# First phase in a new order: the next item's transpositions between the output products, spread and attention products between the value products

## The reference, cut to what matters

```python
q = split_heads(x @ Wq.T); k = split_heads(x @ Wk.T); v = split_heads(x @ Wv.T)   # x: layernormed
q = jax.nn.elu(q) + 1.0
k = jax.nn.elu(k) + 1.0
kv_state = jnp.einsum('bhnd,bhne->bhde', k, v)
k_state = k.sum(axis=2)
attn_out = jnp.einsum('bhnd,bhde->bhne', q, kv_state)
denom = jnp.maximum(jnp.einsum('bhnd,bhd->bhn', q, k_state), 1e-06)[..., None]
attn_out = (attn_out / denom).transpose(0, 2, 1, 3).reshape(b, s, d)
xp = jnp.pad(x, ((0, 0), (1, 1), (0, 0)))
local = xp[:, :-2, :] * conv_w[:, 0] + xp[:, 1:-1, :] * conv_w[:, 1] + xp[:, 2:, :] * conv_w[:, 2] + conv_b
return (attn_out + local) @ Wp.T + bp
```

## Time and profile before

| | us |
|---|---|
| median of three runs | 3675.85 |
| lowest and highest of them | 3665.65, 3680.14 |
| profiled execution | 3669.31 |
| its span | 3667.6 |
| of it TensorE busy | 3419.1 (93%) |
| VectorE busy | 2083.7 (57%) |
| ScalarE busy | 1344.5 (37%) |
| GpSimd busy | 815.0 (22%) |

### The profile page before, as it was taken

How to read it: one execution, slowest core, us unless ns; L and a number is a source line. 1 busy time by engine, 2 the same in 40 slices (tenths; PEclk the granted TensorE clock), 3 DMA queues, 4 the chain that set the end, 5 groups by cost and what they waited for, 6 DMA issues and landing times. The chain is left out here.

```text
span 3667.6 us, 42899 instructions
## 1 busy us (share of the span) xinstructions
PE 3419.1 (93%) x16304; PEld 2809.7 (77%) x16304; DVE 2083.7 (57%) x3935; ACT 1344.5 (37%) x2271; POOL 815.0 (22%) x740
## 2 busy tenths in 40 slices
PE   7999999999849999999999996899999999999798
PEld 6778787878638778877787775788888888888676
DVE  5565656565458888888888885322222223221676
ACT  4444444344235554555555543221111111211232
POOL 2223222232223332333333331000000000000244
PEclk9999999999879999999999998899999999999899
DMA  2010111011031111211121102100000000000343
GB/s 95 35 69 35 69 35 69 35 69 47 35 112 65 52 47 47 82 60 47 47 82 59 47 24 93 45 23 12 12 23 12 13 23 12 23 1 1 118 150 126
DMA packets 102348, 188.37 MB, mean 51 GB/s; under 512 B 6912, under 2 KB 13056, under 8 KB 102144
## 3 DMA queue, kind: packets, MB, share of 16 engines
q1 hardware_dynamic: 99840, 184.58, 14.5%
q10 hardware_dynamic: 2304, 1.05, 0.1%
HBM read 135.28 MB, written 50.33 MB: 51 GB/s over the span
## 5 line engine op out<-in xcount | busy, mean ns | idle before, releaser
L1536 ACT ACTIVATE c_gate<-c_g,c_bias 128x512 f32<-128x512 f32 x192 | 132.4, 689 | 803.1 <-PE c_g L102 803.1
L1555 DVE TENSOR_TENSOR c_gate<-c_gate 128x512 f32<-128x512 f32 x64 | 44.3, 692 | 599.7 <-ACT c_gate L1536 599.7
L1096 DVE TENSOR_TENSOR b_p_lo<-b_p_f,b_p_hi 128x512 fp32r<-128x512 f32 x256 | 255.5, 999 | 55.4 <-ACT b_p_hi L963 52.3
L955 ACT ACTIVATE b_p_f<-b_r,b_p_bias,b_p_scale 128x512 f32<-128x512 f32 x256 | 199.2, 778 | 216.3 <-PE b_r L102 212.6
L256 POOL TENSOR_TENSOR c_ln_sc<-c_ln_ve,minus_half 128x4 f32<-128x4 f32 x16 | 16.1, 1007 | 979.2 <-DVE c_ln_ve L249 979.2
L909 POOL TENSOR_TENSOR b_psum<-b_psum,b_p_f 128x512 f32<-128x512 f32 x128 | 171.2, 1338 | 126.4 <-ACT b_p_f L955 125.1
L1071 DVE CUSTOM_DVE_ANT_0 b_unused<-b_r,b_mask_row 128x512 bf16<-128x512 f32 x256 | 170.3, 683 | 1.2 <-issue 0.6
L963 ACT ACTIVATE b_p_hi<-b_p_f 128x512 fp32r<-128x512 f32 x256 | 161.5, 631 | 18.8 <-ACT b_p_f L955 1.1
L909 POOL TENSOR_TENSOR b_psum<-b_p_f 128x512 f32<-128x512 f32 x64 | 87.5, 1366 | 345.6 <-ACT b_p_f L955 192.5
L915 POOL TENSOR_TENSOR b_q_lo<-b_rope,b_q_hi 128x512 fp32r<-128x512 f32 x64 | 91.3, 1426 | 262.9 <-ACT b_q_hi L973 262.9
L419 POOL TENSOR_TENSOR a_res<-a_res,a_bp 128x512 f32<-128x512 f32 x64 | 81.8, 1308 | 299.9 <-DMA a_res<-in_x 299.9
(11 more groups left out here) (317 smaller groups left out, 10591.6 us busy)
## 6 DMA issues: line engine op xcount, KB each, us to landing
a_x<-in_x SPq DMA_DIRECT2D x16, 1024.0 KB, 8.0
a_res<-in_x SPq DMA_DIRECT2D x16, 1024.0 KB, 5.4
x<-a_res SPq DMA_DIRECT2D x16, 1024.0 KB, 4.3
b_mem<-in_ctx SPq DMA_DIRECT2D x16, 1024.0 KB, 7.8
b_x<-x SPq DMA_DIRECT2D x16, 1024.0 KB, 5.5
b_res<-x SPq DMA_DIRECT2D x16, 1024.0 KB, 5.5
x<-b_res SPq DMA_DIRECT2D x16, 1024.0 KB, 4.3
c_x<-x SPq DMA_DIRECT2D x16, 1024.0 KB, 5.6
```

The source lines that it names most:

```text
L955: act.activation(p_f[:, i, :], bank_of("st", j)[:, :], ACT.Exp, bias=p_bias[:, i:i + 1], scale=p_scale[:, i:i + 1]).then_inc(p_exp.sem, p_ ...
L1096: dve.tensor_tensor(p.low[:, i, :], p_f[:, i, :], p[:, i, :].high_f32(), ALU.subtract).then_inc(p_lo.sem, p_lo.unit)
L1536: act.activation(gate[:, j % 2, i, :], gating.banks[(3 * j + i) % 6][:, :], ACT.Tanh if g == "c" else ACT.Sigmoid, bias=bias[:, i, j:j + 1 ...
```

## The change

The change is a new order on all engines in the first phase; what is computed and the number of instructions of each kind stay.

- TensorE: the transpositions of the next item leave the head of the step. Two of them stand ahead of the first output block, two ahead of the third. They get a ring of their own with two banks (`turning`, names `a_t`), and the ring `second` has three banks instead of four. The first item's transpositions stand ahead of the pipeline. Spread and attention products of chunk c stand ahead of value block c.
- ScalarE: the copies of value blocks (`values`) stand between the spread copies and the high parts of z. High part and middle tap of the next item's chunk 0 stand ahead of the kv high part, those of chunks 1 to 3 behind it.
- VectorE: maximum and reciprocal follow each other directly; low parts and outer taps of the next item stand between the kv low part and the residual additions.
- SyncE: the load of the next x comes first in a step, the load of the residual second.

The core of the diff; helpers that only moved are left out:

```diff
+            turning = Ring(self.banks(ctx, "a_t", 2), [(tap2, c) for c in range(C)], B)
-            second = Ring(self.banks(ctx, "a_r", 4),
-                          [(tap2, c) for c in range(C)] + [e for c in range(C) for e in ((spread_sb, c, 1), (att_sb, c, 1))]
+            second = Ring(self.banks(ctx, "a_r", 3),
+                          [e for c in range(C) for e in ((spread_sb, c, 1), (att_sb, c, 1))]
                           + [(x1_sb, t, 1) for t in range(T)], B)
-            SPREAD, OUT = C, 3 * C
+            SPREAD, OUT = 0, 2 * C
...
                 def step(new, old):
+                    if following(new, B):
+                        load(sp, new.b + 1)
                     if old:
                         if old.b >= 1:
                             sp.wait_ge(stored.sem, stored.upto(old.b - 1))
                         sp.dma_start(res[:, :, :], self.token_rows(io["x"], old.b)).then_inc(res_in.sem, res_in.unit)
-                    if following(new, B):
-                        load(sp, new.b + 1)
...
-                    if old:
-                        for c in range(C):
+                    for c in range(C):
+                        if old:
                             spread_copy(c)
                             if c >= 1:
                                 z_high(c - 1)
+                        if new:
+                            values(c)
+                    if old:
                         z_high(C - 1)
...
+                    if following(new, B):
+                        tokens_high(new.b + 1, 0)
+                        middle_tap(new.b + 1, 0)
...
+                    if after:
+                        tokens_low(after, 1)
+                    if old:
+                        residual(old.b, 0)
+                    if after:
+                        outer_taps(after, 0)
+                        outer_taps(after, 1)
+                    if old:
+                        residual(old.b, 1)
+                    if after:
+                        tokens_low(after, 2)
+                        tokens_low(after, 3)
+                        outer_taps(after, 2)
...
-                    if old:
-                        for t in range(T):
+                    for t in range(T):
+                        if following(new, B) and t % 2 == 0:
+                            turn_x(new.b + 1, t)
+                            turn_x(new.b + 1, t + 1)
+                        if old:
                             if freed := second.freed(s, OUT + t):
                                 pe.wait_ge(*freed)
                             bank = second.bank(OUT + t)
...
+                def turn_x(b, c):
+                    if c == 0:
+                        pe.wait_ge(N.normed.sem, N.normed.upto(b))
+                    if freed := turning.freed(b, c):
+                        pe.wait_ge(*freed)
+                    self.turn(pe, turning.bank(c), x, c).then_inc(xT_ps.sem, xT_ps.unit)
+                for c in range(C):
+                    turn_x(0, c)
                 pipeline(B, step)
```

More of the change, by code:

```diff
@@ L461, in spread_copy, with values @@
                             act.wait_ge(z_lo.sem, z_lo.upto(old.b if c >= 2 else old.b - 1, c - 2 if c >= 2 else C + c - 2))
-                        act.activation(att[c % 2][:, :], second.banks[(SPREAD + 2 * c) % 4][:, :], ACT.Copy).then_inc(spread_sb.sem, spread_sb.unit)
+                        act.activation(att[c % 2][:, :], second.bank(SPREAD + 2 * c)[:, :], ACT.Copy).then_inc(spread_sb.sem, spread_sb.unit)
+                    def values(t):
+                        act.wait_ge(v_ps.sem, v_ps.upto(new.b, t))
+                        if t == 0:
+                            if new.b >= 1:
+                                act.wait_ge(kv_ps.sem, kv_ps.upto(new.b - 1))
+                        act.activation(v1[:, t, :, 0:P],
+                                               first.banks[(V + t) % 3][:, :].rearrange("p (c e) -> p c e", c=C), ACT.Copy).then_inc(v_sb.sem, v_sb.unit)
                     def z_high(c):
@@ L514, in step, with tokens_high, middle_tap @@
                                                 kv_f, ACT.Copy).then_inc(kv_hi.sem, kv_hi.unit)
+                    if following(new, B):
+                        for c in range(1, C):
+                            tokens_high(new.b + 1, c)
+                            middle_tap(new.b + 1, c)
+                def tokens_high(b, c):
+                    act.wait_ge(xT_ps.sem, xT_ps.upto(b, c))
+                    if c == 0 and b >= 1:
+                        act.wait_ge(kq_ps.sem, kq_ps.upto(b - 1))
+                    act.activation(xT.high[:, c, :], turning.bank(c)[:, :], ACT.Copy).then_inc(xT_hi.sem, xT_hi.unit)
+                def middle_tap(b, c):
+                    act.activation(local[b % 2][:, c, :], turning.bank(c)[:, :], ACT.Identity,
+                                   bias=conv_b[:, c:c + 1], scale=conv_w[:, c, 1:2]).then_inc(tap1.sem, tap1.unit)
+                for c in range(C):
+                    tokens_high(0, c)
+                    middle_tap(0, c)
                 pipeline(B, step)
@@ L560, in step @@
                     if new:
-                        taps(1)
+                        elu_back(0)
                         elu_back(1)
@@ L596, in step @@
                                                              bank[:, i, P:P + 1], None, ALU.mult).then_inc(kv_part.sem, kv_part.unit)
+                    after = new.b + 1 if following(new, B) else None
+                    if after:
+                        tokens_low(after, 0)
+                    if new:
                         dve.wait_ge(kv_hi.sem, kv_hi.upto(new.b))
@@ L600, in step @@
                         dve.tensor_tensor(both(kv[new.par].low), kv_f, both(kv[new.par].high).bitcast(F32), ALU.subtract).then_inc(kv_lo.sem, kv_lo.unit)
+                    if after:
+                        tokens_low(after, 1)
                     if old:
-                        for t in range(T):
-                            dve.wait_ge(res_bp.sem, res_bp.upto(old.b, t))
-                            dve.wait_ge(out_ps.sem, out_ps.upto(old.b, t))
-                            dve.tensor_tensor(res[:, t, :], second.banks[(OUT + t) % 4][:, :], res[:, t, :], ALU.add).then_inc(x1_sb.sem, x1_sb.unit)
+                        residual(old.b, 0)
@@ L606, in _, with residual @@
+                def residual(b, t):
+                    dve.wait_ge(res_bp.sem, res_bp.upto(b, t))
+                    dve.wait_ge(out_ps.sem, out_ps.upto(b, t))
+                    dve.tensor_tensor(res[:, t, :], second.bank(OUT + t)[:, :], res[:, t, :], ALU.add).then_inc(x1_sb.sem, x1_sb.unit)
+                for c in range(C):
+                    tokens_low(0, c)
+                    outer_taps(0, c)
                 pipeline(B, step)
@@ L613, in step @@
                     s = new.b if new else old.b + 1
-                    if new:
-                        for c in range(C):
-                            if freed := second.freed(s, c):
-                                pe.wait_ge(*freed)
-                            bank = second.bank(c)
-                            if c == 0:
-                                pe.wait_ge(N.normed.sem, N.normed.upto(new.b))
-                            self.turn(pe, bank, x, c).then_inc(xT_ps.sem, xT_ps.unit)
                     if old:
```

68 lines of the change are left out of this document (27 added, 41 removed).

## The result

| | before | after |
|---|---|---|
| median, us | 3674.97 (four runs, 3665.65 to 3680.14) | 3709.18 (four runs, 3707.69 to 3709.27) |
| profiled execution, us | 3669.31 | 3709.27 |

The changed kernel takes 1.0091 of the time before, 95% interval 1.0074 to 1.0109: slower by 0.9%, as forecast (3708). The interval holds no 1, so the sign is clear of the noise.

The account below looks back on a forecast made before the run. TensorE was taken to set the pace, losing 4.03 us of each 59.67 us pass. 3669.3 + 1.0 + 12.7 - 0.7 + 22.4 = 3704.7, stated as a median of 3708 us; range 3692 to 3720, 8 in 10 3672 to 3732.

Parts of the forecast that it names:

- start and second pass: First transpositions have only two banks, so two tap pairs (2.9 us) precede the fourth chunk; with the second pass, +1.0 us.
- last pass and drain: The last pass, which holds only the old item, was to stay as before: 0.
- What the change removes: Stops between key and value products, at the spread and attention products, go: up to 4.03 us a pass given back.
- Wait (a): Late value copies, z splits and normalisation delay the first query block; the fourth waits 0.7 us for its PSUM bank.
- Wait (b), (c): Late query chain starts kv masks 3.4 us behind key-value products; third and fourth transpositions await taps' banks, 4.2 us lost.
- The clock: TensorE runs about 8 products at 1.2 GHz behind the new stop: 1.6 us a pass, 22.4 us in all.
- The store and the loads: SyncE's later residual load delays GpSimd's bias additions, but value products cover that: costed at 0, 14 us if uncovered.
- Rival 1: The clock holds through the stop, all else as forecast: 3686 us, no change; chance 0.20.
- Rival 2: VectorE's chain to the taps is shorter: 3655 us, or 3614 if taps are wholly in time; chance 0.14.
- Rival 3: The clock falls deeply at each stop, 2.9 us a pass: 3726 us with the median's offset; chance 0.13.
- rival 4: The spread stretch still stops for its 2.8 us a pass: 3747 us; chance 0.04.

Follow-up runs that it names:

- interleaving alone: Kernel before with only spread and attention products ahead of each value block and ScalarE's value copies among them; 3633.19 us, ratio 0.9889 to before.
- statistics early: Changed kernel with the next item's normalisation statistics ahead of the last low part of z on VectorE; 3657.38 us, ratio 0.9956 to before.
- Later turns: Changed kernel with chunk 2's transpositions ahead of the fourth output block, chunk 3's behind it, VectorE's low part 3 behind residual 2; 3640.31 us, ratio 0.9907 to before.
- Taps before the residual: Changed kernel with residual addition 0 behind the first two pairs of taps on VectorE; 3690.64 us, ratio 1.0034 to before.
- the old order: Changed kernel with SyncE's loads in their old order, residual first, then next x; 3711.26 us, ratio 1.0100 to before.
- another start: Changed kernel with two fills of unused tiles on VectorE ahead of the first phase's very last residual addition; median 3706.66 us, ratio 1.0077 to before.
- both repairs: Changed kernel with the edits of Later turns and statistics early together; 3618.28 us, ratio 0.9837 to before.

## Why the prediction was right, point by point

The ledger of the two profiled executions, whose spans lie 39.9 us apart, against the forecast's 35.4:

| part | forecast | measured |
|---|---|---|
| start and second pass | +1.0 | +3.7 |
| the 14 passes, clock included | +34.4 | +29.0 |
| last pass and drain | 0 | -1.4 |
| rest | 0 | +8.6 |

- **What the change removes** held. No spread or attention product waits in any of the 14 passes, and the two waits of the earlier trace rows are gone. The interleaving alone brings 2.3 us of the 4.03 a pass; 1.06 us (9.3 + 5.6 in 14 passes) stays idle in its passes, for the reciprocal's low part, which was waited for before, and for the fourth query block, which is new.
- **Wait (a)**, forecast 0.7: the query products take 11.60 to 11.64 us instead of 10.88, 13 times. It comes with the interleaving alone (5.6 us, 13 times), and statistics early removes it, so its cause is shown: value copy, z high, z low, normalisation, first query block.
- **Wait (b), (c)**: masks 3.4 us behind the key-value products, measured 3.26; stop 4.2, measured 570.06 - 564.9 - 0.83 = 4.33. It is made up otherwise than forecast: 2.95 us up to the third transposition, and from there 2.21 us to the first product, 0.83 of it work at the full clock, where the forecast had a second wait of 1.0. The transpositions run slow, so that only 0.34 us of that wait is left between them. Later turns removes this stop alone, statistics early shortens it: the mechanism is shown from both ends.
- **The clock** is the term that was mis-sized in the passes. I took 1.6 us for 8 slow products behind each stop. Where eight are slow, that is the price (statistics early: passes of 60.1 us with eight against 58.5 without), but it is not paid at each stop. In ten passes only two or three are slow (570.06 to 571.06), and the second half of the outputs takes 6.25 us instead of 5.61; the last four have 10, 7, 5 and 12 slow ones. The mean is 0.97 us, so this term was 8.8 us too large over 14 passes. Taps before the residual shows that the size could not have been read from the length of the stop alone.
- **Start and second pass**, forecast +1.0. The stops ahead of the first key products (3.28 and 0.92 us) were foreseen, but the first key product starts 4.0 us later (34.61 against 30.59), where I had 2.9. I had not foreseen that nine products behind them would be slow (34.61 to 38.17): the key products of the first item take 12.99 us instead of 12.34. The second pass's denominator starts 1.2 us later than these two explain, where I had 0.9. And this pass has wait (a) already, 0.7 us, which I counted from the third pass on. Together the error is 2.7 us.
- **The store and the loads**, forecast 0: the old order gives the same pass, 61.73.
- **What the sum left untouched** was not untouched: the rest took 8.6 us more. I had costed it at nothing since no instruction of it changes. The counts of slow products show the clock in the second phase as its cause: 130 against 67, with nearly equal waits. The new order does not force them, since three kernels that keep it in the main (statistics early, another start, taps before the residual) took 2625.7, 2618.1 and 2622.2 us. Nor are they plain noise: the unedited kernels repeated their 2634.2 and 2625.9. Yet one kernel may vary as well, as the two groups of times of another start suggest. What picks one course or the other is not settled.

So 3708 against 3709.18 is closer than the sum deserves. The direction follows from the mechanism that the runs show; the closeness is luck. The clock in the passes was too dear by 8.8 us and the last pass by 1.4; stops 2.1, start 2.7 and rest 8.6 were too cheap, and 1.3 us lie in stages that this ledger does not separate. A slip of the sum is in it too: 60.55 - 59.67 = 0.88, times 14 is 12.3 us, not 12.7.

Rival 1 fell: the clock did drop at every stop, if less. (With a shorter stop, in statistics early, it held in ten passes of 14.) Rival 2 fell as well; every link of the chain came within 0.25 us. But its second number, 3614 for a change whose taps are in time, is what both repairs together give (3618.28). Rival 3 fell with the 0.97 us, and rival 4 with the spread stretch.

## What to carry to other kernels

When work is moved between engines' orders, take each wait that the new place needs and follow it through the queue of the engine that must answer it, with all that stands ahead there: here the gain on TensorE was sure, and two banks that VectorE freed late cost 4.3 us a pass, and the clock behind them 1.0, and ate it. A ring made shorter is gated by its last reader's place in line; where a moved consumer must wait, moving it one or two blocks further (later turns, 69 us less) or filling the answering engine's idle time (statistics early, 52 less) can be worth more than the change itself. Of these 52 us, 8.6 came from phases that the edit does not touch, so a whole time alone would have misled. And a change of several parts is to be taken apart: half of this one was worth -1.1%.

## What the runs showed of the hardware that was not expected

- **A stop and the clock behind it can trade.** With the stop 0.6 us shorter (first wait 2.11 us instead of 2.70), the slow products went from 56 to 71 in 14 passes and most passes stayed at 61.4 us. The Trainium skill ("TensorE: Matmul & The Clock Gate", A second HAM failure mode: psum-queue depth-cycling) describes a kernel that idles in small pieces and pays for re-throttling between bursts; the trace agrees for the stops of 2.70 and 0.34 us, but the idle 0.42 us ahead of the fourth query block bring no slow product, and no run here ties the number of slow products to the idle time.
- **The same stop can cost clock or not.** In statistics early, waits of 1.5 and 0.8 us with four transpositions between are followed by eight slow products in four passes and by none in ten, 1.55 us apart. There the clock falls only when TensorE is at work again (136.69), while in after it is down at the third transposition already.
- **The same three untouched phases take 2618 to 2634 us.** The waits of TensorE in the second phase hold 86 to 88 us in each kernel, but its slow products number 45 to 131. A kernel repeated its own value within 0.3 us in a second profile, and a later start alone does not set it. A comparison of whole times at half a per cent can hold 16 us of that.
- **Equal passes do not make equal times.** After stayed within 3703 to 3709 in ten runs. The kernel with two fills has the same passes in its profile and spread over 3693 to 3720 in six. The kernel before, whose passes vary from 58.4 to 61.0 us, spread over 3662 to 3692 in 44.
